# State space stage of a decoder: product start condition, projection of C as rows, held features turned in front of the output product

## What is computed

```python
xz = x @ W_in                          # (256, 1024): features and gate
xc = conv(xz[:, :512], conv_w, 4 taps) # full 512 x 512 per tap
u = silu(xc + conv_b)
dt, Bm, Cm = split(u @ W_x, [128, 16, 16])
delta = softplus(dt @ W_dt + b_dt)
h[t, n] = exp(delta * A[n]) * h[t-1, n] + delta * u * Bm[t, n]   # 16 states n
y = sum_n(h[t, n] * Cm[t, n]) + D * u
out = layernorm(x + (y * silu(gate)) @ W_out + held)             # held: the convolved features
```

## Time and profile before

| | us |
|---|---|
| median of 3 runs | 2904.63 (2903.69 to 2905.1) |
| the profiled execution, its own time | 2909.72 |
| its span in the trace | 2907.4 |
| the state space stage's scans, first to last start | 1704.5 to 2325.2 |

### The profile page before, as it was taken

How to read it: one execution, slowest core, us unless ns; L and a number is a source line. 1 busy time by engine, 2 the same in 40 slices (tenths; PEclk the granted TensorE clock), 3 DMA queues, 4 the chain that set the end, 5 groups by cost and what they waited for, 6 DMA issues and landing times. The chain is left out here.

```text
span 2907.4 us, 47462 instructions
## 1 busy us (share of the span) xinstructions
PE 2623.1 (90%) x16930; PEld 1760.0 (61%) x16941; DVE 1988.6 (68%) x2548; ACT 1459.1 (50%) x2864; POOL 1206.2 (41%) x1148
## 2 busy tenths in 40 slices
PE   8999899988888888887999999999998879998997
PEld 5666655634444444443899777777776555555873
DVE  4788757689999999966121149999999933333544
ACT  3444422279999998972232156666676511111520
POOL 0000026446665665553222137776888810000352
PEclk9999999989999999999999999999999989998899
DMA  2123514268888888975012201111112270120273
GB/s 94 57 91 128 190 56 116 58 134 171 168 164 171 169 167 160 189 161 188 30 39 72 102 37 52 59 59 59 59 52 81 85 130 23 43 81 8 98 153 146
DMA packets 537722, 297.99 MB, mean 102 GB/s; under 512 B 444400, under 2 KB 482544, under 8 KB 533680
## 3 DMA queue, kind: packets, MB, share of 16 engines
q1 hardware_dynamic: 520896, 258.50, 35.4%
q0 software_dynamic: 16624, 36.84, 4.1%
HBM read 126.45 MB, written 64.23 MB: 66 GB/s over the span
## 5 line engine op out<-in xcount | busy, mean ns | idle before, releaser
L1188 DVE TENSOR_REDUCE xh_top<-xh_seen 128x1 f32<-128x512 f32 (+1 forms) x768 | 631.6, 864 | 44.1 <-PE xh_seen L1090 30.5
L1160 ACT ACTIVATE xh_prob<-xh_sc,xh_bias,xh_scale 128x1024 int16<-128x1024 f32 (+1 forms) x512 | 610.1, 1202 | 67.4 <-PE xh_sc L1090 67.1
L2335 POOL TENSOR_TENSOR ss_state<-ss_du,ss_b_all 128x1024 f32<-128x1024 f32 x128 | 433.3, 3395 | 185.2 <-PE ss_turned L1933 110.8
L1090 PE MATMUL xh_seen<-xh_kT,xh_qT 96*128 96x512 bf16 x1024 | 353.3, 387 | 80.4 <-DVE xh_top L1188 78.1
L2383 DVE TENSOR_TENSOR_SCAN ss_state<-ss_decay,ss_state 128x1024 f32<-128x1024 f32 x128 | 386.9, 3023 | 28.7 <-ACT ss_decay L2185 28.7
L1090 PE MATMUL xh_sc<-xh_kT,xh_qT 96*128 96x512 bf16 x1024 | 308.1, 383 | 1.4 <-ACT xh_prob L1160 1.3
L1214 POOL CAST xh_probT<-xh_pairs 128x2048 int16<-128x2048 uint8 x128 | 242.1, 1891 | 12.6 <-DMA xh_pairs<-xh_prob 3.8
L1090 PEld LDWEIGHTS xh_seen<-xh_kT,xh_qT 96*128 96x128 bf16 x1024 | 89.2, 97 | 240.8 <-DVE xh_top L1188 219.2
L1940 PE MATMUL ss_bank<-ss_xc,hold_w_conv 128*128 128x256 f32 x1024 | 229.3, 379 | 0.7 <-ACT ss_xc L2197 0.7
L2185 ACT ACTIVATE ss_decay<-ss_delta,ss_a 128x255 f32<-128x255 f32 x512 | 210.7, 496 | 0.4
L1940 PEld LDWEIGHTS ss_bank<-ss_xc,hold_w_conv 128*128 128x128 f32 x1024 | 190.0, 189 | 26.4 <-ACT ss_xc L2197 1.1
(11 more groups left out here) (399 smaller groups left out, 4767.8 us busy)
## 6 DMA issues: line engine op xcount, KB each, us to landing
ex_rows_in<-sa_unused POOLq DMA_DIRECT2D x18, 1088.0 KB, 5.2
ss_b_all<-ss_states SPq DMA_DIRECT2D x8, 2048.0 KB, 7.2
xa_kT<-xp_kT SPq DMA_DIRECT2D x8, 768.0 KB, 5.2
xh_qT<-xa_qT SPq DMA_DIRECT2D x48, 128.0 KB, 3.2
xh_kT<-xa_kT SPq DMA_DIRECT2D x48, 128.0 KB, 3.4
sa_x<-in_x SPq DMA_DIRECT2D x8, 512.0 KB, 3.8
sa_y<-in_x SPq DMA_DIRECT2D x8, 512.0 KB, 6.6
x_after_self_attention<-sa_y_out SPq DMA_DIRECT2D x8, 512.0 KB, 6.1
```

Source lines behind the costliest of these rows:

```text
L1090: ins = pe.matmul(out[:, c * D:(c + 1) * D], qT[s][:, t * P:(t + 1) * P], kT[s][:, at + c * D:at + (c + 1) * D], start=True, stop=True)
L1160: act.activation(out, scores, ACT.Exp, bias=bias[t % RING][:, :], scale=scale[s][:, t:t + 1], accum_out=total[s][:, half, t:t + 1]).then_i ...
L1188: ins = v.tensor_reduce(top[t % RING][:, k:k + 1], scores[:, 0:n], AX.X, ALU.max)\
L2335: g.tensor_tensor(state[k % RING][:, :, :], du[s][:, :, :], spread(b_all[s][:, k, :], KD), ALU.mult)\
```

## The change

Three edits, all in `state_space`.

1. Products wait for a scan. `drive` for chunk c, for all chunks from 4 on, waits after `turn_ready` also for `scanned` of chunk c-3.
2. C is projected together with B as rows. The four products for B give 32 rows (B and C) where they gave 16, ACT copies 32 rows to `b_rows`, and at k = 9 PE turns them with two transposes, whose C half ACT copies to `c_t` in k = 9. The eight products of k = 8 are gone. PE at k = 9 waits for ACT's copy of `b_rows`.
3. In `y_half` the four `held` blocks are transposed (transpose mode, first in the bank), and the four products with `w_out` are added after them.

```diff
@@ y_half
                     for c in range(KD):
-                        pe.matmul(out[:, :], outT[:, c, t * P:(t + 1) * P], w_out[:, c, :], start=(c == 0), stop=False)
+                        pe.matmul(out[:, c * P:(c + 1) * P], held[:, c, t * P:(t + 1) * P], ident[:, :],
+                                  is_transpose=True, start=(c == 0), stop=False, skip_group_check=True)
                     for c in range(KD):
-                        ins = pe.matmul(out[:, c * P:(c + 1) * P], held[:, c, t * P:(t + 1) * P], ident[:, :],
-                                        start=False, stop=(c == KD - 1))
+                        ins = pe.matmul(out[:, :], outT[:, c, t * P:(t + 1) * P], w_out[:, c, :], start=False,
+                                        stop=(c == KD - 1), skip_group_check=True)
@@ piece, k == 8
-                                ins = pe.matmul(out[0:N, S:2 * S], w_x[:, c, DT:DT + N], u[:, c, :],
+                                ins = pe.matmul(out[0:2 * N, S:2 * S], w_x[:, c, DT:DT + 2 * N], u[:, c, :],
                                                 start=(c == 0), stop=(c == KD - 1))
                             full(ins, DT_B)
-                            out = fill(C_T)
-                            for t in range(TB):
-                                for c in range(KD):
-                                    ins = pe.matmul(out[:, t * N:(t + 1) * N], u[:, c, t * P:(t + 1) * P],
-                                                    w_x[:, c, DT + N:DT + 2 * N], start=(c == 0), stop=(c == KD - 1))
-                            full(ins, C_T)
@@ piece, k == 9, in front of y_half(1, Y1)
+                        if mid:
+                            wait_read(pe, q, s, DT_B)
+                            out = fill(C_T)
+                            pe.sem_inc(pe_waited, 1)
+                            for t in range(TB):
+                                ins = pe.transpose(out[:, t * 2 * N:(t + 1) * 2 * N], b_rows[:, t * P:(t + 1) * P],
+                                                   ident[0:2 * N, 0:2 * N])
+                            full(ins, C_T)
@@ scalar, k == 8, and now k == 9 for the copy to c_t
-                        copy(b_rows[:, :], src[0:N, S:2 * S], DT_B)
+                        copy(b_rows[:, :], src[0:2 * N, S:2 * S], DT_B)
+                    if k == 9 and mid:
                         src = wait_filled(act, q, s, C_T)
-                        copy(flat(c_t[1 - s][:, :, :]), src[:, 0:TB * N], C_T)
+                        copy(c_t[1 - s][:, :, :], src[:, 0:TB * 2 * N].rearrange("p (t n) -> p t n", t=TB)[:, :, N:], C_T)
@@ gpsimd, drive
                     if not (isinstance(q, int) and c < RING):
                         g.wait_ge(turn_ready, ONE + (c - RING + 1) * TB)
                         g.sem_inc(waited, 1)
+                        g.wait_ge(scanned, ONE + c - DRIVE_LEAD + 1)
+                        g.sem_inc(waited, 1)
```

More of the change, by code:

```diff
@@ L1730, in state_space @@
         y_done = p.sem("y_done"); offset_ready = p.sem("offset_ready"); chain_y = p.sem("chain_y"); waited = p.sem("waited")
-        v_waited = p.sem("v_waited")
+        v_waited = p.sem("v_waited"); pe_waited = p.sem("pe_waited")
         ctx_here = [p.sem(f"ctx_here{i}") for i in (0, 1)]; keys_ready = p.sem("keys_ready")
@@ L1794, in state_space @@
         dt = p.sb("dt", [P, S])
-        b_rows = p.sb("b_rows", [N, S])
+        b_rows = p.sb("b_rows", [2 * N, S])
         b_all = [p.sb(f"b_all{s}", [P, N, S]) for s in (0, 1)]
@@ L1879, in step @@
                         sp.wait_ge(b_in, ONE + 16 * n)
-                    sp.dma_start(slot.rearrange("o (n t) -> (o n) t", t=S), b_rows[:, :]).then_inc(b_out, 16)
+                    sp.dma_start(slot.rearrange("o (n t) -> (o n) t", t=S), b_rows[0:N, :]).then_inc(b_out, 16)
                     sp.wait_ge(b_out, ONE + 16 * (n + 2))
@@ L2010, in piece @@
                             for c in range(KD):
-                                ins = pe.matmul(out[0:N, S:2 * S], w_x[:, c, DT:DT + N], u[:, c, :],
+                                ins = pe.matmul(out[0:2 * N, S:2 * S], w_x[:, c, DT:DT + 2 * N], u[:, c, :],
                                                 start=(c == 0), stop=(c == KD - 1))
                             full(ins, DT_B)
-                            out = fill(C_T)
-                            for t in range(TB):
-                                for c in range(KD):
-                                    ins = pe.matmul(out[:, t * N:(t + 1) * N], u[:, c, t * P:(t + 1) * P],
-                                                    w_x[:, c, DT + N:DT + 2 * N], start=(c == 0), stop=(c == KD - 1))
-                            full(ins, C_T)
                         else:
                             pass_over(DT_B)
+                    elif k == 9:
+                        if mid:
[6 more added lines that the diff above has]
+                            full(ins, C_T)
+                        elif not (static and n == B - 1):
                             pass_over(C_T)
-                    elif k == 9:
                         if post:
```

## The result

The changed kernel took 2924.4 us in the median of 4 runs (2918.41 to 2926.86), the kernel before 2904.86 (4 runs, 2903.69 to 2905.42): 1.0065 times as long, with an interval of 1.0047 to 1.0082. It is slower by 19.5 us, and above the range of the forecast. The profiled execution took 2926.11 around a span of 2924.0, against 2909.72 around 2907.4: +16.6 us of span. The other 3 us of the median lie between the executions: the profiled one of before lay 4.9 us above its median, that of after only 1.7. I work with the spans from here on.

The account below looks back on a forecast made before the run. It took a loop of waits, with DVE's scans and POOL's products excluding each other, as the bound. Terms -0.75 + 2.5 + 3.6 - 0.8 + 2.1 - 0.9 = +5.75 us gave 2910.4 us, range 2901 to 2919.

Parts of the forecast that it names:

- rival (a): PE's longer wait at chunk 13 lowers its clock in each batch: +6 us in five batches, 2916 us; chance 0.2.
- the signs that were named: Products of 2.36 us behind scans, scans of 3.4, POOL's busy time down, PE's down 2.4 a batch, chunk 13 waits over 4.
- batch 0: Nine products of chunks 7 to 15 each 0.3 us later, +2.7, less 0.2 taken up by a wait for ACT: +2.5 us.
- batches 2, 4, 5, 6: Chunks 12 and 14 delay scans 10 and 12, 0.6, plus 0.3 not absorbed from chunks 0 to 2: +0.9 each, +3.6 us.
- batches 1, 3: Product 12 follows scan 9, so scan 10 loses 0.9 us less; with +0.3 to +0.6 for waits, -0.4 each, -0.8 us.
- start of the stage: In the first step Z no longer waits behind the C products and starts at 1689.4 instead of 1690.12: -0.75 us.
- end of the stage: Behind the last scan both halves of `y` are on the path and get cheaper with transposes: -0.9 us.
- Release from DVE to POOL took 0.08 us: Products released by a scan's end start about 0.1 us later and need 2.36, ending 0.3 us later (0.28 to 0.41).
- its "against": Argument against the clock falling in each batch: the loop's DVE part is now longer and hides a bit.
- (b): DVE's 3.0 us of waits for ACT absorb the products' 0.3 in full batches: +2 us, 2907 us; chance 0.12.
- (c): Scan 8 starts ahead of product 10 and gains up to 1.8 us on the loop: 2900 to 2905 us; chance 0.15.
- (d): The wait costs nothing; only the stage's ends and batches 1 and 3 remain: -2.5 us, 2902 us; chance 0.08.

Follow-up runs that it names:

- f1: The changed kernel plus three overwritten products ahead of the gate's at k = 13, so that PE waits less at chunk 13; stage 636.4 us, ratio 1.0052.
- h2: The changed kernel with products waiting for DVE's work just ahead of scan c-3 instead of for that scan; stage 620.4 us, ratio 1.0000.
- g3: The changed kernel with products released later, by the first half of the adding up behind scan c-3; stage 668.2 us, one run of 2984.19 us.
- e2: The kernel before with only the products' wait for scan c-3 added; stage 636.8 us, ratio 1.0066.
- g2: The changed kernel with the wait for scan c-3 only on products of states 3 to 15; stage 638.5 us, ratio 1.0065.
- g1: The changed kernel with the wait for scan c-3 only on products of states 0 to 2; stage 626.4 us, ratio 1.0033.
- h1_one_product: The changed kernel without its wait, but product 12 waits for the statistics DVE takes just ahead of scan 9; stage 614.4 us, ratio 0.9987.
- e1: The changed kernel without the products' wait for scan c-3, its other two edits kept; stage 622.9 us, ratio 1.0012.

## Why the prediction was wrong

**The steps that failed.** The sum gave the clock nothing: the cost of more falls stood beside it as rival (a), for the case that replaces the forecast, when it came on top. And it priced a product released by a scan's end at 0.3 us, when it costs 0.38. The sum missed 10.9 us. Of these, 5.8 go in batches 1 to 6 of the kernel that removes the falls there (f1), some 2 us (an estimate) are the price, 0.08 a product, and 1.3 lie in stages that the change doesn't touch.

**Right in kind.** That scans and products exclude each other, that the wait changes no order but turns held products into released ones, that PE's savings lie outside the loop, and that the wait makes the stage slower, all hold. The Trainium skill ("SBUF — State Buffer", "Who interferes with whom") says that the order of issue decides who blocks; the trace agrees, and h2, the changed kernel and g3 show what it leaves to the programmer: the same order costs 0, 0.38 or 1.0 us a scan by the moment of the release. The profile showed most of the signs that were named: products of 2.36 at a scan's end, scans near 3.4, POOL's group down by 64 us. Two were missed: PE's busy time did not fall (in batch 4 it rose from 75.48 to 76.92 us), and its wait at chunk 13 stayed under 4 us.

**Term by term**, forecast against measured (us of the span):

| term | forecast | measured |
|---|---|---|
| batch 0 | +2.5 | +4.07 |
| batches 2, 4, 5, 6 | +3.6 | +9.22 |
| batches 1, 3 | -0.8 | +1.23 |
| batch 7 | +2.1 | +1.93 |
| start of the stage | -0.75 | -0.42 |
| end of the stage | -0.9 | -0.73 |
| stages ahead | 0 | +1.30 |
| sum | +5.75 | +16.6 |

1. *The price of a release.* The step "Release from DVE to POOL took 0.08 us" took the only such row, from another stage, and priced a product at 0.3, with 0.41 as its upper end. It is 0.18, and the price 0.18 + 2.36 - 2.16 = 0.38. In batches 2, 4 and 5 the step on the wait was off by little: without a fall of the clock (f1) they took 1.1 us more than before, against the forecast's 0.9. Batch 6 took 1.65 more. In batch 0 ten scans took 3.47 and not nine 3.4, and none of it was absorbed: 10 x 0.38 = 3.8 of the 4.07.

2. *The clock.* Rival (a) was not an alternative to the forecast, it came on top of it. PE's wait at chunk 13 grew to 3.3 us, less than the 4.5 worked out, and the clock fell there ahead of each of batches 1 to 6. Taking f1's batches as those without a fall (an estimate, as the filling moves products too; e2 and g2 give 0.8 and 1.5 for a fall of 3.4 us), the falls cost 0.80, 2.30, 0.88 and 0.31 us in batches 2, 4, 5 and 6, 4.3 of the 6 that the rival gave. It failed in its "against", that the loop's DVE part hides a bit, and in its chance. It also doesn't need the transposes: e2_wait_only has none of the new ones and its clock falls too, so nothing here bears on whether transposes count for the clock.

3. *Batches 1 and 3.* The forecast gave them -0.4 each, because product 12 would no longer stand ahead of scan 10. That came true (no scan of them takes 4 us any more), but it is worth less than was said: without the falls f1 took 79.67 and 79.65 there against 79.87 and 79.72, -0.2 and -0.1. And the falls stayed, at 0.77 and 0.73 by the same comparison. The step took the order of the instructions for the whole effect of the fall.

4. *The ends.* At the start PE went on 3.22 us after the beginning of the B product instead of 3.64. Start of the stage in the changed kernel on PE, from the B product to Z:

```profile
1687.78 1.91 PE L2012 MATMUL ss_bank<-ss_u,ss_w_x 128*32 128x256 f32 x8
1690.51 0.28 PE L2023 MATMUL ss_bank<-ss_ident,ss_b_rows 32*128 32x32 f32 x2 [0.82 <-ACT ss_b_rows L2201]
1691.00 0.89 PE L2039 MATMUL ss_bank<-ss_dt,hold_w_dt 128*128 128x256 f32 x3 [0.21 <-PEq L1923]
```

The forecast let Z follow the copy by 0.3 us; it left out PE's pass from the copy's end (1690.37) to the transposes, 0.14, and the 0.21 behind them. The end of the stage gave 0.73 of 0.9. The +1.3 of earlier stages isn't touched by the change; I take it for the scatter of single executions, which isn't shown.

**Rivals (b), (c), (d).** (b) underrated the full batches: only the fronts' products are absorbed (g1). (c) came in part and brought nothing to be seen: in batches 4 and 5 scan 8 fell from 4.04 and 4.03 us to 3.48 and 2.61, yet both took longer than before, each behind a fall of the clock of 6.8 us. Its idea, that PE's saving can win through another order, is what h1_one_product shows at product 12. (d) is refuted by every row of 3.47.

**The range** ended at 2919, made for (a) alone on top of a price of 0.3. The upper ends of the unknown costs were known (0.41 a product, a longer fall, as the one of 6.8 us that batch 7 of before already had) and would have had to be added to (a), not set beside it.

## What to carry to other kernels

Where two engines exclude each other, the waiter should be released by the work just ahead of the blocking instruction, so that it is started and held; released by the blocker's end, it pays the release latency each time, here 0.38 us a scan. Price such a latency from a row of the same pair of engines in the same kind of work, and add up rivals that don't exclude each other: a longer wait of PE brought the extra latency and the slower clock together. And PE time saved outside the loop of waits moves only the order in which others start, which can be worth more, either way, than the time itself: -0.2 us for the stage in e1, -8.7 with one product held in place (both against the one trace of before).

## What the runs showed of the hardware

- A POOL product that has started and is held by a scan ends 2.17 us after the scan; one released by the scan's end starts 0.18 us behind it and ends 2.54 behind. The held one is not only spared the release, its own 2.36 shrinks by 0.19.
- A product holds small DVE instructions too: a TENSOR_SCALAR of 128x2 took 1.63 us behind one (h1) and 0.17 without (h2).
- The granted clock fell to half for 3.4, 6.8 or 10.2 us around PE's waits for DVE. The length of the wait alone doesn't tell which: in e2 one wait of 2.44 us had a fall and the next of 2.44 had none, in g2 a wait of 3.33 had none and others of 3.3 had one. A fall of 3.4 us cost 0.8 us a batch in e2, 1.5 in g2 and nothing in h2.
